# A transformer layer on one core: score products on two row tiles of TensorE, and a new order of all steps

## What is computed

```
x: (4, 1024, 256)                       # four batch items, 1024 positions, 256 channels
mod = silu(c) @ wmod                    # six rows of 256 for each item: sa ca ga sb cb gb
h = layernorm(x) * (1 + ca) + sa
q, k, v = h @ Wq + bq, h @ Wk + bk, h @ Wv + bv     # 4 kv heads of 16 channels
q, k = rope(q), rope(k)
att = softmax(where(causal, q . k / sqrt(d), -inf))
x = x + ga * ((att @ v) @ Wo + bo)
h = layernorm(x) * (1 + cb) + sb
x = x + gb * block(h)                   # routed gated MLP, 704 hidden channels
```

## Time and profile before

| what | value |
|---|---|
| median of the runs | 466.64 us (465.21, 466.64, 467.13) |
| span of the profiled execution | 466.8 us |
| granted TensorE clock, mean | 0.990 |
| busy: PE, PEld, DVE, ACT, POOL | 437.2, 371.8, 353.9, 308.4, 182.2 us |
| matmul records | 3320 |

### The profile page before, as it was taken

One profiled execution on the slowest core, in us unless ns is written; L12 is line 12 of the kernel. 1 busy time (PEld: TensorE's weight loads), 2 busy tenths in 40 slices (PEclk: granted clock), 3 DMA queues, 4 the chain that ended last, 5 costly groups with the idle time before them and its releaser, 6 DMA issues. The chain is left out here.

```text
span 466.8 us, 9486 instructions
## 1 busy us (share of the span) xinstructions
PE 437.2 (94%) x3320; PEld 371.8 (80%) x3320; DVE 353.9 (76%) x796; ACT 308.4 (66%) x640; POOL 182.2 (39%) x262
## 2 busy tenths in 40 slices
PE   5887979888989999999999999999999999999996
PEld 5674545686587688997858999999898798999995
DVE  4579968788989488898855889888885766578565
ACT  2298578775588887527697764676768698645441
POOL 6376527410246220214827404523243333325622
PEclk9999899999999999999999999999999999999998
DMA  7921030000000100020021000000010000000001
GB/s 192 333 93 51 3 97 1 2 1 3 0 3 11 43 2 0 2 70 1 27 86 24 2 1 24 1 26 5 20 51 9 24 22 2 25 1 24 22 25 46
DMA packets 16576, 16.04 MB, mean 34 GB/s; under 512 B 4233, under 2 KB 14926, under 8 KB 16530
## 3 DMA queue, kind: packets, MB, share of 16 engines
q1 hardware_dynamic: 16530, 15.44, 10.8%
HBM read 11.09 MB, written 4.21 MB: 33 GB/s over the span
## 5 line engine op out<-in xcount | busy, mean ns | idle before, releaser
L792 PE MATMUL banks<-gTh,guhi 128*128 128x256 f32 x352 | 101.2, 287 | 0.0
L794 PE MATMUL banks<-gTh,gulo 128*128 128x256 f32 x352 | 98.8, 281 | 0.0
L793 PE MATMUL banks<-gTl,guhi 128*128 128x256 f32 x352 | 98.7, 280 | 0.0
L937 ACT ACTIVATE PT<-banks 128x1024 f32<-128x1024 f32 (+3 forms) x96 | 74.5, 810 | 29.8 <-PE banks L708 24.4
L792 PEld LDWEIGHTS banks<-gTh,guhi 128*128 128x128 f32 x352 | 66.4, 189 | 1.6 <-issue 0.7
L1165 DVE TENSOR_REDUCE mxp<-banks 128x2 f32<-128x1024 f32 (+3 forms) x56 | 61.9, 1141 | 6.4 <-PE banks L684 3.9
L793 PEld LDWEIGHTS banks<-gTl,guhi 128*128 128x128 f32 x352 | 66.5, 189 | 0.3
L794 PEld LDWEIGHTS banks<-gTh,gulo 128*128 128x128 f32 x352 | 66.4, 189 | 0.0
L684 PE MATMUL banks<-QKT 128*128 128x512 f32 (+3 forms) x192 | 49.9, 368 | 6.8 <-ACT QKT L915 3.4
L708 PE MATMUL banks<-QKT 128*128 128x512 f32 (+3 forms) x192 | 50.9, 369 | 0.9 <-ACT PT L937 0.4
L708 PEld LDWEIGHTS banks<-QKT 128*128 128x128 f32 x192 | 30.3, 190 | 23.3 <-issue 21.2
(11 more groups left out here) (178 smaller groups left out, 1093.4 us busy)
## 6 DMA issues: line engine op xcount, KB each, us to landing
xres<-in_L_attn_x SPq DMA_DIRECT2D x8, 512.0 KB, 4.4
out_x<-xres SPq DMA_DIRECT2D x16, 256.0 KB, 2.1
wm_st<-in_L_wmod SPq DMA_DIRECT2D x1, 1024.0 KB, 7.9
modB<-mod_scratch SPq DMA_DIRECT2D x4, 256.0 KB, 3.4
wg_st<-in_L_ffn_w_gate SPq DMA_DIRECT2D x1, 704.0 KB, 5.0
wu_st<-in_L_ffn_w_up SPq DMA_DIRECT2D x1, 704.0 KB, 6.2
xres<-in_L_ffn_w_down SPq DMA_DIRECT2D x1, 640.0 KB, 5.7
wm_st<-in_L_wmod SPq DMA_DIRECT2D x1, 512.0 KB, 6.2
```

What stands on the lines that cost most here:

```text
L792: pe.matmul(out_, guhi[:, k, blk, :], gh, start=(m == 0 and k == 0), stop=False)
L793: pe.matmul(out_, guhi[:, k, blk, :], gl, start=False, stop=False)
L794: i = pe.matmul(out_, gulo[:, k, blk, :], gh, start=False, stop=(m == len(blocks) - 1 and k == KB - 1))
L937: act.activation(PT[:, u % 2, 2 * q:2 * q + 2, 0:CH - q0], both("prob", b, n)[:, :, 0:CH - q0], ACT.Exp, scale=float(D) ** -0.5).then_inc( ...
```

## The change

Two things are changed. In max and prob steps that carry a mark (an apostrophe behind the word in ORDER), the matmul of head e reads only the 64 partitions of that head, of the weights and of the moving operand. Both heads' matmuls then lie on two different row tiles of the array, 64*128 each. 91 steps are marked: 69 of the 96 prob steps (21, 19, 16 and 13 in the four items) and 22 of the 80 max steps (4, 6, 8 and 4), all of the latter with 512 keys, one query block and no mask. The other steps stay as they were. And the list ORDER is written anew from end to end, bank numbers included; the same steps stand in it, each as often as before.

```diff
+def rows_of(kind, b, n, e):
+    return slice(e * HR, (e + 1) * HR) if (kind, b, n) in ON_ROWS else slice(0, P)
...
 ORDER = """
-prob0 rstd1 wol norm1 wo5 x1 rstd2 norm1 norm1 norm2 exp exp norm1 prob6 exp prob2 prob0 pv5 prob6 exp wo2 pv exp exp
...
+exp prob4' exp prob0' wob rstd2 exp pv3 norm2 prob6' exp prob4' pv exp wo0 exp prob6' x1 pv exp prob4' exp pv rstd2
...
+        tiled, word = word.endswith("'"), word.rstrip("'")
...
+        if tiled:
+            ON_ROWS.add((kind, s // per, s % per))
...
                         for e in range(2):
-                            i = pe.matmul(o[:, e, m * kn:(m + 1) * kn], QKT[:, q, qt * P:(qt + 1) * P],
-                                          QKT[:, 2 + 2 * q + e, k0:k0 + kn], start=(m == 0),
+                            rows = rows_of(kind, b, n, e)
+                            i = pe.matmul(o[:, e, m * kn:(m + 1) * kn], QKT[rows, q, qt * P:(qt + 1) * P],
+                                          QKT[rows, 2 + 2 * q + e, k0:k0 + kn], start=(m == 0),
...
                     for e in range(2):
-                        i = pe.matmul(o[:, e, 0:CH - q0], QKT[:, 2 + 2 * q + e, j * P:(j + 1) * P],
-                                      QKT[:, q, c * CH + q0:(c + 1) * CH], start=True, stop=True)
+                        rows = rows_of(kind, b, n, e)
+                        i = pe.matmul(o[:, e, 0:CH - q0], QKT[rows, 2 + 2 * q + e, j * P:(j + 1) * P],
+                                      QKT[rows, q, c * CH + q0:(c + 1) * CH], start=True, stop=True)
```

More of the change, by code:

```diff
@@ L119 @@
[L119 to L138, removed]
@@ L144 @@
[L144 to L153, removed]
@@ new lines @@
+sil up1 up2 fft up6 sthi fft h2hi stlo yT2 ffhi qkv0 ytm ffhi ffl xev gate1 fflo h2lo sil stack4 qkvb stk fft qkv7
+stack0 qkvb ms1 max4 rope ffhi rs1 max6 stk gate3 mxr sil gate2 mxr sthi stlo max6 sil max4 max0 mxr up3 mxr fft up6
+stack4 mxr stk down3 fflo fft ffhi max4 sum ffhi ffl max6' mxr max2' max0 mxr ynT4 down5 ynev mxr mxr gate4 sum mneg
+fin fflo max0' sil max2' mxr mtT5 stack6 mrow mxr mrd wo4 stk gate5 store x1 max2 sil rstd2 max6' mxr ldx max4' up0
+mxr max2 mxr max6 gate1 fft mxr sil up0 mxr ffhi fflo up6 wo7 fft max2' ffhi mxr max4' down0 woh ffl fft mxr ffhi
@@ new lines @@
+prob2 a1 sum exp route prob4 down0 x1 exp prob2 ms2 rstd2 sum prob4 exp max6 fflo exp max0 pmask mxr a2 pmask mxr
+prob4' fin prob6' pv3 route pv exp wol exp prob0' prob4' ms2 down2 ldW pmask mneg exp store exp rs2 stats pmask h2 pv
+h2 pv sum rstd1 hT4 ycopy mtT2 wob hhi h2T5 mrow yT3 hlo down0 norm1 ytm h2hi norm1 mrd norm1 norm1 sum a4 h2lo ynT1
+fin route a0 ynev prob2' route exp prob4 prob6' norm2 exp store prob0' ldG prob2' exp pv4 exp wo5 ldx prob6' exp x1
+prob0' pv exp xT2 exp rstd2 pv xev prob0' prob6' exp prob2' qkv5 stats exp exp prob0' prob6' rstd1 pv ms2 ms2 gate2
@@ new lines @@
+exp rs2 exp pmask xT3 h2 hT6 h2 pmask pv hhi norm1 ms1 hlo prob0' rs1 pv exp xev h2T6 prob0 norm1 norm2 gate7 exp
+norm1 h2hi norm1 sil prob0 h2lo up3 pmask ldB exp a6 fft a2 route ms2 xT3 prob0 route qkv6 exp xev pmask pv pv up2
+qkvb sil qkvb fft up5 ffhi up6 ycopy fflo ms2 rope ms1 yT4 rs1 hT7 hhi qkv2 sthi rs2 ytm gate3 h2 stlo h2 gate4 sil
+fft sil gate0 qkvb sil hlo h2T1 wo7 x1 h2hi xT0 ffhi up2 ffhi ffl xev h2lo stack4 rstd2 fft qkv7 ffhi fflo stk fft
+stack0 fflo down6 qkvb ffhi rope stk ffl ynT7 max4 ynev sum max0 mxr sthi max6 mxr wo4 max2 mxr down5 mxr sum gate2
@@ L167 @@
+h2T2 fft gate0 h2hi h2lo ffhi ffl fflo up3 sil up2 fft ffhi gate3 fflo gate0 sil fft gate3 ffhi sil fflo up2 sil up0
+fft down1 ffhi fft ffl ffhi sum down0 fflo down1 sum fin fin down0 sum store sum store
 """.split()
+ON_ROWS = set()
 def steps():
```

68 lines of the change are left out of this document (41 added, 27 removed).

## The result

The changed kernel takes 470.89 us (median; 468.73 to 472.00), against 466.44 us for the kernel before on the same chip: 1.0097 times the time, with a 95% interval of 1.0068 to 1.0127. It is 4.5 us slower, where 6.4 us of gain were forecast. The same file on another chip gave 1.013 (1.009 to 1.017). Both lie above the predicted range, by 0.9 us the first, and on the wrong side of no change.

The account below looks back on a forecast made before the run. PE was taken as the bound, full after 160 us. Row tiles' 18.3 us less 10.5 us of switches was to bring 4.3 + 1.6 + 0.5 = 6.4 us to the end: 460.2 us, range 453 to 470.

Parts of the forecast that it names:

- What bounds the kernel: PE full from 160 to 460 us, 93% busy from 100 to 160; DVE, then PE and ACT, before 100 us.
- Rival 3: Third and fourth items: PE's saving turns into waits for other engines, a third of 4.3 us left; 463 to 467 us; 0.12.
- What a row tile saves: Marked max and prob steps: two heads' matmuls run beside each other and cost one, saving 18.3 us of PE time.
- Rival 5: Marked steps: the two matmuls do not run beside each other, nothing is saved; 474 to 476 us; 0.09.
- What a switch costs: Changing the array's division drains it and uncovers a load: 0.17 us each, 62 added, 10.5 us in all.
- Rival 2: Switches to row tiles free or nearly so: about 453 us, half free 456; 0.14.
- rival 4: Loads cannot run ahead on a computing row tile: 41 marked steps uncover 0.107 us each, 4.4 us; 464 to 465; 0.07.
- The balance of a lone run: Marked 512-column steps among whole-array matmuls: one saves 0.23 and pays 0.34, losing 0.1 us; two together gain 0.12.
- The first item: Its 25 marked steps save 4.8 less 3.2 us of PE time; beside DVE and ACT bounds, 0.5 us was taken.
- What is only moved: New list holds the same steps on each engine, so other work does not change: 0 with 3 us either side.
- The case: A new list whose new waits cost more than 5 us: 467 to 472 us; 0.08.
- What would show it: Profile signs: pairs under 0.02 us apart, two marked steps in 0.67 us, idle weight loads, PE busy 10 to 16 us less.

Follow-up runs that it names:

- three later items' chosen marks: Kernel before, list kept, with 52 marks where a run saves more than its switches, none in the first item: 463.94 us, ratio 0.9945 to the kernel before.
- mended new list: Changed kernel with ten PE steps given other banks, one norm2 step moved behind a row maximum, first item unmarked (66 marks): 466.98 us, ratio 1.001 to the kernel before.
- old_list_all_marks: Kernel before, list kept, with all 128 steps marked that can be: 467.64 us, ratio 1.0029 to the kernel before.
- new_list_no_lone_runs: Changed kernel with 39 marks taken off, wherever a run of marks does not touch pv, 52 left: 470.87 us, ratio 1.0098 to the kernel before.
- old_list_marks: Kernel before, list kept, with the same 91 steps marked as in the changed kernel: 464.93 us, ratio 0.9995 to the kernel before.
- old_list_chosen_marks: Kernel before, list kept, with 77 marks only where a run saves more than its switches: 463.44 us, ratio 0.9944 to the kernel before.

## Why the prediction was wrong, point by point

**What bounds the kernel.** PE after 160 us, and DVE and ACT before 100: right for the kernel before. "There whatever PE is spared comes off the time, as long as the others keep up" carried the condition that failed. In the old list the three later items' chosen marks give 2.6 us of 4.8; in the mended new list 66 marks give 0.84%, 3.9 us, of the 6.1 that their working had. By the traces' 0.19 us a switch 0.7 to 0.9 us of each gap is the dearer switch, and the rest went into waits. Rival 3, other engines take PE's place, is what happened in part, at places where DVE's result was already just in time.

**What a row tile saves.** Right. The two matmuls start within 7 ns of each other in 84 of 91 pairs and take the time of one. Rival 5 is out.

**What a switch costs.** Nearly right: 0.17 forecast, 0.17 to 0.20 in the traces, 0.19 by old_list_all_marks. On the 62 added switches that is some 1.2 us more than the 10.5 forecast. Rival 2 (free) is out. So is rival 4: the middle step of the run of three at 372.68 takes 0.231, so loads do run ahead on a row tile that is computing. The rule in "TensorE: Matmul & The Clock Gate", Part 3, of the Trainium skill, that a load overlaps matmuls in flight only when its row group differs, is not borne out by these rows.

**The balance of a lone run.** Right in sign, shown by new_list_no_lone_runs (no difference) and old_list_all_marks (slower). A lone step loses nearer 0.16 us than 0.1, and two together gain 0.07 rather than 0.12.

**The first item.** 0.5 us was forecast. Nothing was gained, in either list. That DVE and ACT bound it was right; that marks could go with a lower clock there was not thought of. With them the mean clock of the runs was 0.984 and 0.977, without them 0.992, and in the old list 0.989 against 0.994. The new list without any mark had 0.989, though, so the list has a part in it.

**What is only moved.** This is the step that failed. "I see no reason for a sign and give it 0 with 3 us to either side": it costs 8.6 to 8.8 us. The argument was that the steps are the same, so the work is. But an order decides more than the work: which bank a step gets and who reads it last, how much stands between the start of a chain (mtT) and its user (prob), what stands ahead of a reader in DVE's queue. The banks and the distances stand in the list and could have been looked at before the run. The case had 0.08 and a band of 467 to 472, which holds the result; it deserved the most thought, since the change rewrites all 58 lines of the list, and the list was the part that the prediction did not walk through. The same paragraph says that a wait is hidden from 100 us on by the mix with the MLP. That failed too: PE idles for 7.7 us after 160 us with this list and no mark, where it was 2.6.

**The gain itself.** It was put at 6.4 us and measured at 2.5 to 4.1 in the new list, the second step that failed: the dearer switches, the first item's 0.5 us that did not come, and savings that turned into waits.

**Its own time.** "The median of the runs is 0.2 below the profiled span" mixed two things. A run's time is its span and about 1.7 us, so the median execution of the kernel before has a span near 464.9, and the profiled one, 466.8, was a slow one. The number 460.2 was still the median less 6.4, so nothing came of it.

**What would show it.** Of the signs named, the pairs, the 0.67 and the idle weight loads came true. PE's busy time was to fall by 10 to 16 us: it did not fall in the changed kernel, and by 4.1 us in old_list_marks and 6.9 in old_list_chosen_marks (437.2 to 433.1 and 430.3). That number is a poor sign in any case, as it also moves with the clock. "The forecast is wrong if PE idles for over 5 us after 160 us" is the one that came true: 9.1 of 300 us, where it was 2.6, and 7.7 of it by the list without a mark.

The sum, by ratios on 466 us: the list +8.6, the marks -2.5 to -4.1, together +4.5 to +6.1.

## What to carry to other kernels

A rewritten order is a change of its own: walk through it on the engine that bounds, for every step whose buffer has a late reader, and time the order without the feature before the two are judged together. Two row tiles are a real gain for products over 64 rows, but here each change of the array's division cost 0.17 to 0.20 us, so mark only runs that save more than their two switches. Where the bound engine is full but its partners are just in time, count on half to two thirds of what is saved: 2.6 of 4.8 and 3.9 of 6.1 us here.
